# A hyperbolic attention layer with an fp8 feed-forward: a new slot table for the shared PSUM bank, with most uses split around the values matmuls

## What is computed

```python
q_h, k_h, v_h = exp_map_at_origin(split_heads(xn @ W.T), c)      # tanh(|v|) * v/|v|
arg    = max(1 + 2c |q-k|^2 / ((1 - c|q|^2)(1 - c|k|^2)), 1 + EPS)
scores = -beta_pos * arccosh(arg) / sqrt(c) - attention_bias
out    = softmax(scores) @ log_map_at_origin(v_h)                # per head
x      = x + concat(log_map(exp_map(out))) @ W_o.T
x      = x + bf16(fp8(layernorm(x)) @ fp8(kernel)) + bias
```

## Time and profile before

| | us |
|---|---|
| median of 3 runs | 2432.06 |
| lowest, highest | 2428.98, 2432.98 |
| the profiled execution | 2433.24 |
| its span from the first to the last instruction | 2431.4 |
| ACT busy in it | 1937.7 (80%) |
| PE busy in it | 1945.1 (80%) |
| DVE, POOL busy in it | 970.8 (40%), 362.6 (15%) |
| mean granted clock of PE | 0.809 |

### The profile page before, as it was taken

How to read it: one execution, slowest core, us unless ns; L and a number is a source line. 1 busy time by engine, 2 the same in 40 slices (tenths; PEclk the granted TensorE clock), 3 DMA queues, 4 the chain that set the end, 5 groups by cost and what they waited for, 6 DMA issues and landing times. The chain is left out here.

```text
span 2431.4 us, 29241 instructions
## 1 busy us (share of the span) xinstructions
PE 1945.1 (80%) x10317; PEld 624.6 (26%) x10317; DVE 970.8 (40%) x2289; ACT 1937.7 (80%) x1184; POOL 362.6 (15%) x223
## 2 busy tenths in 40 slices
PE   4458897989888768888879489798979888888682
PEld 2222232323222222222323123232323222222221
DVE  4432344343534345343444534443343534221413
ACT  1039999998989659998989389899988989999491
POOL 1111121121212002020212102121121212010011
PEclk9959798988888778897989579898888888876675
DMA  1120101001010200202020020201001010200000
GB/s 37 57 57 10 49 10 51 25 19 58 18 58 1 66 9 11 65 1 75 1 66 10 1 75 1 66 10 66 10 18 58 18 49 1 66 1 18 1 18 10
DMA packets 79154, 75.58 MB, mean 31 GB/s; under 512 B 34651, under 2 KB 60508, under 8 KB 78940
## 3 DMA queue, kind: packets, MB, share of 16 engines
q1 hardware_dynamic: 78940, 73.02, 9.6%
HBM read 17.96 MB, written 55.05 MB: 30 GB/s over the span
## 5 line engine op out<-in xcount | busy, mean ns | idle before, releaser
L911 ACT ACTIVATE U<-ps 128x2048 f32<-128x2048 f32 x500 | 939.0, 1878 | 178.6 <-PE ps L820 169.3
L916 ACT ACTIVATE U<-U,sc 128x2048 f32<-128x2048 f32 x512 | 1025.4, 2003 | 0.0
L820 PE MATMUL ps<-q_T,k_T 18*128 18x512 f32 x4096 | 750.4, 770 | 222.7 <-ACT U L911 149.2
L833 PE MATMUL ps<-U,vals 128*32 128x512 f32 x4096 | 680.6, 743 | 50.1 <-ACT U L916 29.1
L820 PEld LDWEIGHTS ps<-q_T,k_T 18*128 18x128 f32 x4096 | 224.5, 218 | 756.0 <-ACT U L911 592.5
L340 PE MATMUL ps<-wT,xnT 128*128 128x384 f32 x512 | 231.7, 581 | 13.7 <-DVE qkv L370 9.4
L370 DVE COPY qkv<-ps 128x384 f32<-128x384 f32 x128 | 71.4, 558 | 342.4 <-PE ps L340 334.8
L306 POOL TENSOR_TENSOR sqr<-qkv 128x768 f32<-128x768 f32 x64 | 94.1, 1470 | 732.4 <-DVE qkv L370 651.2
L833 PEld LDWEIGHTS ps<-U,vals 128*32 128x32 f32 x4096 | 87.9, 118 | 327.7 <-ACT U L916 216.6
L348 PE MATMUL ps<-ident,rows 128*128 128x128 f32 x512 | 99.2, 325 | 84.6 <-POOL rows L323 66.6
L340 PEld LDWEIGHTS ps<-wT,xnT 128*128 128x128 f32 x512 | 98.3, 213 | 161.5 <-issue 107.2
(11 more groups left out here) (174 smaller groups left out, 1336.3 us busy)
## 6 DMA issues: line engine op xcount, KB each, us to landing
q_scratch<-q_T SPq DMA_DIRECT2D x16, 1024.0 KB, 4.5
k_scratch<-k_T SPq DMA_DIRECT2D x16, 1024.0 KB, 6.9
v_scratch<-vals SPq DMA_DIRECT2D x16, 768.0 KB, 10.9
xt<-in_L_attn_x_dram SPq DMA_DIRECT2D x16, 512.0 KB, 3.8
fi_xt<-in_L_attn_x_dram SPq DMA_DIRECT2D x16, 512.0 KB, 4.7
out_dram<-fi_x SPq DMA_DIRECT2D x16, 512.0 KB, 3.2
rk_scratch<-rk SPq DMA_DIRECT2D x16, 32.0 KB, 12.2
wraw<-in_L_attn_W_q_dram SPq DMA_DIRECT2D x1, 256.0 KB, 2.9
```

The source lines that it names most:

```text
L820: ins = pe.matmul(g.ps[:, 2 * pair + i, :], a.k_T[HB * h:HB * h + RD, b % 2, hg, kt * P:(kt + 1) * P], a.q_T[HB * h:HB * h + RD, G % 3, hg ...
L833: ins = pe.matmul(g.ps[HB * h:HB * h + VW, 6, :], a.vals[:, b % 2, kt, (hg * HPG + h) // 2, DH * (h % 2):DH * (h % 2) + VW], U[:, n % RING ...
L911: act.activation(U[:, n % RING].rearrange("p b n -> p (b n)"), chunk(n), ACT.Ln, scale=-2.0 / EPS, bias=1.0).then_inc(ln_done, 1)
L916: act.activation(U[:, n % RING], U[:, n % RING], ACT.Exp, scale=g.NEGB).then_inc(exp_done, 1)
```

## The change

Two tables and the rules that read them change; no arithmetic is added or left out. `BOTH` marks a use that is cut in two on PE: its first half of instructions ahead of the values matmuls, the second half behind them; the semaphore that DVE waits for is raised by the second half alone, and the copy counts as one of half 1. The projection stage has 36 slots in place of 32 and begins four steps sooner (`EARLY`): slot k now stands at step s = k - 4, slots 0 to 3 at steps 28 to 31 of the group before. X comes to steps 0 and 1, M to steps 3 to 8, 11 and 13, R to steps 23 to 31, W to 12 and 15, Q to 21, both Y to 22. The slots of the small instructions move along. Steps 14, 16, 17, 19 and 20 have no use now; before these were 0, 1, 17, 20 and 23.

```diff
-PROJECT_USES = {("X", 0): (3, 0), ("X", 1): (4, 0),
-                ("M", 0): (5, 0), ("M", 1): (6, 0), ...
...
+BOTH = 2
+EARLY = 4
+SLOTS = 36
+PROJECT_USES = {("X", 0): (4, BOTH), ("X", 1): (5, BOTH),
+                ("M", 0): (7, BOTH), ("M", 1): (8, BOTH), ...
...
-    steps_before = {0: 0, 2: 8, 20: 12, 22: 17}
+    steps_before = {0: 0, 2: 8, 21: 12, 23: 17}
...
-        if k in (6, 8, 14, 16):
+        if k in (9, 11, 13, 18):
...
-        if k == 23:
+        if k == 24:
             pool.wait_ge(small_rdy, n + 1)
...
-    steps_before = {5: 0, 7: 1, 13: 5, 15: 13, 17: 20}
+    steps_before = {5: 0, 7: 1, 16: 5, 18: 13, 20: 20}
...
-            for dc in range(2):
+            for dc in halves(part, range(2)):
...
-        ins.then_inc(a.b7_filled, 1)
+        if part != 0:
+            ins.then_inc(a.b7_filled, 1)
...
+        def projected(G, s):
+
+            return [(n, k) for n, k in ((G + 2, s + EARLY), (G + 3, s + EARLY - STEPS))
+                    if n < NG and 0 <= k < SLOTS]
...
+                    both = [(kind, m, i) for m, k in projected(G, s) for kind, i in begun(PROJECT_USES, k)]
+                    if G >= 1:
+                        both += [(kind, G - 1, i) for kind, i in begun(FINISH_USES, s)]
                     for key in in_step(G, s, 0):
                         use(*key)
+                    for key in both:
+                        use(*key, 0)
                     if n >= 1:
                         values(n - 1)
                     for key in in_step(G, s, 1):
-                        use(*key)
+                        use(*key, 1 if key in both else None)
```

More of the change, by code:

```diff
@@ L242, in at, with begun, halves @@
 def at(table, slot, half):
-    return [key for key, where in table.items() if where == (slot, half)]
+    return [key for key, where in table.items() if where == (slot, half) or (half, where) == (1, (slot, BOTH))]
+def begun(table, slot):
+    return [key for key, where in table.items() if where == (slot, BOTH)]
+def halves(part, items):
+    items = list(items)
+    return items if part is None else items[:len(items) // 2] if part == 0 else items[len(items) // 2:]
 def project_stage(nc, ctx, g, a, uses):
@@ L325, in gpsimd, with tensor @@
                                    ALU.mult).then_inc(rows_rdy, 1)
-    def tensor(pe, n, key):
+    def tensor(pe, n, key, part=None):
         kind, i = key
         bank = g.ps[:, 7, :]
-        if uses.before((kind, n, i)):
-            pe.wait_ge(a.b7_copied, uses.before((kind, n, i)))
+        if part != 1:
+            if uses.before((kind, n, i)):
+                pe.wait_ge(a.b7_copied, uses.before((kind, n, i)))
+            if kind == "X" and i == 0:
+                pe.wait_ge(xn_rdy, n + 1)
+            if kind == "R" and i % HG == 0:
+                pe.wait_ge(rows_rdy, 2 * n + i // HG + 1)
+                pe.wait_ge(small_rdy, n + 1)
         if kind == "X":
-            if i == 0:
-                pe.wait_ge(xn_rdy, n + 1)
-            for t in range(GT):
+            for t in halves(part, range(GT)):
                 ins = pe.transpose(bank[:, t * P:(t + 1) * P], xt[:, t, i * P:(i + 1) * P], g.ident[:, :])
@@ L343, in tensor @@
             qk, hg = i // HG, i % HG
[L344 to L348, removed]
+            for t in halves(part, range(GT)):
+                ins = pe.transpose(bank[:, t * P:(t + 1) * P],
+                                   rows[:, qk, t, hg * HPG:(hg + 1) * HPG, :].rearrange("p h r -> p (h r)"),
                                    g.ident[:, :])
@@ L555, in gpsimd, with tensor @@
                                ALU.add).then_inc(yb2_rdy, 1)
-    def tensor(pe, n, key):
+    def tensor(pe, n, key, part=None):
         kind, i = key
         bank = g.ps[:, 7, :]
-        if uses.before((kind, n, i)):
-            pe.wait_ge(b7_copied, uses.before((kind, n, i)))
+        if part != 1:
+            if uses.before((kind, n, i)):
+                pe.wait_ge(b7_copied, uses.before((kind, n, i)))
+            if kind == "T" and i == 0:
+                pe.wait_ge(oc_rdy, n + 1)
+            if kind == "Q":
+                pe.wait_ge(xq_rdy, n + 1)
         if kind == "T":
-            if i == 0:
-                pe.wait_ge(oc_rdy, n + 1)
-            for t in range(GT):
+            for t in halves(part, range(GT)):
                 ins = pe.transpose(bank[:, t * P:(t + 1) * P],
@@ L568, in tensor @@
         elif kind == "W":
-            for a in range(2):
+            for a in halves(part, range(2)):
                 t = 2 * i + a
@@ L574, in tensor @@
         elif kind == "Q":
-            pe.wait_ge(xq_rdy, n + 1)
-            for dc in range(2):
+            for dc in halves(part, range(2)):
                 for t in range(GT):
@@ L724, in emit_layer @@
             for half in range(2):
-                for key in before_steps(k, half):
+                for key in use_before_steps(k, half):
                     uses.add(key)
@@ L771, in _ @@
                 for k in range(LEAD):
-                    for n in range(2):
-                        if 0 <= k - PROJECT_LAG * n < 32:
-                            project.sync(sp, n, k - PROJECT_LAG * n)
+                    for n, slot in before_steps(k):
+                        project.sync(sp, n, slot)
                 finish.sync(sp, 0, 0)
@@ L843, in turn_sums, with use @@
                     ins.then_inc(a.b7_filled, 1)
-                def use(kind, n, i):
+                def use(kind, n, i, part=None):
                     if kind == "S":
```

99 lines of the change are left out of this document (52 added, 47 removed), and 5 rows, old and new, of the table PROJECT_USES.

## The result

| | before | after |
|---|---|---|
| median, us | 2432.06 | 2442.01 (five runs, 2438.68 to 2444.28) |
| ratio | | 1.0044, 95% interval 1.0024 to 1.0063 |
| profiled execution, its span | 2433.24, 2431.4 | 2442.01, 2440.1 |
| first Ln at | 161.0 | 152.5 |
| ordinary group (mean of eleven) | 132.8 | 132.2 |

The mean clocks are those of the profiled executions and don't tell the two kernels apart: over all executions it was 0.788 to 0.813 before and 0.787 to 0.808 after.

A forecast was written before the change was run, and what follows sets the result against it. ACT was taken to set the pace at 3.65 us a step, with stalls and PE's half clock losing 16.4 us a group. Eleven ordinary groups -76, group 8 -5, lead-in +2 gave -79: 2353 us, range 2318 to 2404.

The forecast's parts named there:

- the X and R 0 stalls: PE and ACT waits at step 3 for the layernorm and step 24 for POOL's rows; both go, R 0's worth 3.1 us.
- step 29 of 1.1: ACT's pair L407, L409 with its wait moves to step 29 and costs about 1.1 us.
- steps 16 to 25: New waits and half clock from about step 17 cost 7.3 us a group against 6.7 now: loss 0.6.
- The split: Dividing a use costs PE one exposed weight load, 0.21 us, making an M step 3.76; bounds 0 to 0.6.
- Rival 4: The split makes PE the slower bound, deciding from 0.75 us per M and W on: 2494 us, chance 0.08.
- The clock from step 23 through 13: PE's granted clock stays at 1.00 from step 23 through step 13 of the next group.
- Q and Y: Y 0 at step 22 waits for Q's copy behind DVE's chains: 2.5 us taken, bounds 0.4 to 4.6.
- The sum: An ordinary group gains 7.1 + 0.4 - 0.6 = 6.9 us, 126.3 in place of 133.2; eleven of them 76.
- The others: Groups 5, 15, 0 and 14 net 0, group 8 net -5, the slots ahead of step 0 +2 us.
- Rival 1: Transposes don't hold the clock, which falls at about step 1 as before; a group gains 1.3: 2416 us, chance 0.13.
- Rival 2: DVE's backlog, a late copy of Q, holds Y, R 0 and distances 6 to 7 us: 2398 us, chance 0.15.
- Rivals 3 and 5: 3: clock hardly falls, steps 16 to 25 cost 4, 2318 us, chance 0.10. 5: new order, old times, 2430, 0.04.

The follow-up runs named there:

- e1: The changed kernel with every divided use undivided again, the new slots kept: 2356.22 us, ratio 0.9672 to the kernel before.
- e10: The changed kernel with R 4 at step 28 alone undivided: 2404.09 us, ratio 0.9878 to the kernel before.
- e11: e7 with the quantising chain's two additions made by DVE, directly behind L682, instead of by POOL: 2304.51 us, ratio 0.946 to the kernel before.
- e7: e1 with the finish stage's two small DVE instructions for the maximum moved from slot 20 to 24: 2304.35 us, ratio 0.9481 to the kernel before.
- e12: e11 with six idle transposes added in each of steps 14, 16, 17, 19 and 20: 2270.53 us, ratio 0.9335 to the kernel before.
- e8: e7 with six idle transposes added in each of steps 14, 16, 17, 19 and 20: 2290.73 us, ratio 0.9418 to the kernel before.

## Why the prediction was wrong

*What bounds the kernel; the X and R 0 stalls.* Right in the main, though the 178.6 us held 25.7 ahead of the first Ln, and were not the only large idle time of ACT: the open Ln have 116.8. Steps 2 to 5, which lost 5.7 us a group, lose nothing, and PE no longer waits for layernorm or rows in an ordinary group. The slots alone bring 2356.22 us (e1), where 2353 was forecast for slots and division together, and an ordinary group of 126.25 where the sum gave 126.3. The agreement is partly luck: e1 has no step 29 of 1.1 (it is 0.34) and more at steps 16 to 25 (8.2 against 7.3).

*The split: the step that failed.* It was priced as time on PE: one weight load, 0.21 us for each M. That price was right. M to M after, both halves of M 1 and the first of M 2:

```profile
1446.58 0.91 PE L360 MATMUL ps<-wT,xnT 128*128 128x384 f32 x2
...
1448.42 0.91 PE L360 MATMUL ps<-wT,xnT 128*128 128x384 f32 x2
...
1450.34 0.91 PE L360 MATMUL ps<-wT,xnT 128*128 128x384 f32 x2
```

3.76 us, 3.76 forecast, and no step from 7 to 12 is longer than 3.65. But the division also moves the end of the fill behind the values, and with it the copy (1.06 to 2.43 us behind the Ln), and with that all that DVE has queued behind the copy. The prediction saw this at W 1 (0.7 expected, 0.90 measured) and did not ask it of M 2 and R 4, where the same order stands: "the finish stage's pair at step 6 costs 0.5" measured 1.18, of it 0.7 this wait. Rival 4, the one rival on this term, looked at PE too, and its condition (0.75 us per M) was never met; the kernel became slower by another path.

*The clock from step 23 through 13: failed.* Forecast 1.00 throughout; it is half from step 30.9 to 1.8, which costs 2.8 us at steps 30 to 1 (table, after). Most of this hangs on R 4's late copy, which lengthens step 29 by 0.63 us: with R 4 alone undivided (e10) the half clock there lasts 6.8 in place of 13.7 us in group 9, and steps 30 to 1 lose 1.0 on the mean of the eleven.

*Steps 16 to 25.* The fall came where it was put, at step 17.6, ACT waits at step 16, and Y 0 waits 1.50 us for the copy of Q. The size was wrong, 10.2 us in place of 7.3, just beyond the 10 that was to prove it wrong. By terms, taking steps 16 to 18 for ACT's pairs and W 1, 19 to 21 for the clock and S, and 22 to 25 for Q and Y: 2.4 (2.95 forecast), 2.0 (1.9) and 5.8 against 2.5. So the term mis-sized is Q and Y, beyond its upper bound of 4.6. From the sums of step 18 to the copy of Q DVE took 17.8 us (1503.19 to 1520.96), where 15 were forecast. The first chain and the maximum took about what was forecast, 4.4 and 2.3, but the second chain took 7.9 us (1509.31 to 1517.25) and not 6.7, and a gap of 1.38 at the branch of the unit (L1083) stood ahead of the maximum. The 6.7 of the earlier trace rows already held one such wait for POOL, since its first row took 2.13 us and the same instruction takes 0.22 after; by itself the chain is 4.8 us long (e11). This term owes nothing to the division (5.6 in e1); e7 shows its size, 3.0 us less without the maximum there.

*The sum.* Forecast for an ordinary group 9.5 us lost, measured 15.4: steps 16 to 25 +2.9, steps 30 to 1 +2.8, step 6 +0.7, step 29 -0.2, W -0.3. Times eleven that is 65 of the 88 us between forecast and profiled execution; 5 more come from taking group 9's 133.2 for the mean of 132.8, and 18 from the other groups and the lead-in.

*The others.* Groups 5, 8 and 15 were forecast at 0, -5 and 0 and came at +6.5, +3.7 and +5.2; without the division they are at -3.3, -3.5 and -0.7. Groups 0 and 14, forecast at 0, lost 4.1 and 4.5; most of that is there without the division too (+4.0 and +2.6), steps at half clock, and its cause was not tested further. The lead-in gave 8.5 where +2 was forecast. It can be chance: e11 and e12, whose code is the same up to group 1, have their first Ln at 156.8 and 148.6 in their profiled executions, 8.2 us apart, and e7 and e8 at 153.7 and 157.8.

*Rival 1, transposes don't hold the clock:* fell, though the clock did fall ahead of steps 0 to 1, near the place it named. e8 adds nothing but transposes, and the half clock at steps 18 to 22 is gone in eight of eleven groups. Its price had also been added up wrongly: of 7.1, less 4.5 for X, X and S and 2.5 for M, 0.1 is left and not 1.5, which would have put it at about 2431 and not 2416. The sentence of the Trainium skill ("TensorE: Matmul & The Clock Gate", Part 4) that transposes do not count as PE being busy is not borne out by these rows. *Rival 2, the backlog:* right in its place and nearly in its size, 5.8 us against the 6 to 7 it named, and alone it would not have made the kernel slower. *Rivals 3 and 5:* fell.
